# A decoder layer on Trainium2: queries moved into the stacked layout as one tile and then three

## The reference

```python
qkv = jnp.einsum('bsd,ed->bse', x, Wqkv_w) + Wqkv_b
q = qkv[..., :D_MODEL]
k = qkv[..., D_MODEL:D_MODEL + HEAD_DIM]
v = qkv[..., D_MODEL + HEAD_DIM:]
q = q.reshape(B, S, HEADS, HEAD_DIM)
scores = jnp.einsum('bqhd,bkd->bhqk', q, k) * scale
scores = jnp.where(causal[None, None], scores, min_val)
attn = jax.nn.softmax(scores, axis=-1)
ctx = jnp.einsum('bhqk,bkd->bqhd', attn, v)
...
x = x + _L0_attn_ref(_layernorm(x, axis=-1), ...)
x = x + _L0_xattn_ref(_layernorm(x, axis=-1), fside_BxS2xS2_0, ctx_1024)
x = x + _L0_ffn_ref(_layernorm(x, axis=-1), ...)
```

## Time and profile before

| | us |
|---|---|
| median of 3 runs (941.45 to 944.6) | 943.83 |
| the profiled execution | 943.11 |
| its span in the profile | 941.4 |
| PE busy in it | 902.0 |
| DVE / ACT / POOL busy | 552.4 / 338.5 / 309.5 |

### The profile page before, as it was taken

One profiled execution on the slowest core, in us unless ns is written; L12 is line 12 of the kernel. 1 busy time (PEld: TensorE's weight loads), 2 busy tenths in 40 slices (PEclk: granted clock), 3 DMA queues, 4 the chain that ended last, 5 costly groups with the idle time before them and its releaser, 6 DMA issues.

```text
span 941.4 us, 13548 instructions
## 1 busy us (share of the span) xinstructions
PE 902.0 (96%) x5191; PEld 667.7 (71%) x5191; DVE 552.4 (59%) x897; ACT 338.5 (36%) x577; POOL 309.5 (33%) x419
## 2 busy tenths in 40 slices
PE   3989998899999999999999999999999999999998
PEld 2756567655578886766688767766778778688886
DVE  2635558888557777654757768644577654422223
ACT  4333633545734153254433161434234332121110
POOL 3535733247731241235501333152323141011110
PEclk9977999899999999999999999999999999999999
DMA  9867854545856634356248334373444445265442
GB/s 310 266 207 256 301 190 129 171 142 211 307 224 175 218 129 150 130 201 240 117 174 251 134 106 161 132 290 108 163 159 162 168 180 206 91 242 194 170 179 95
DMA packets 44964, 175.07 MB, mean 186 GB/s; under 512 B 7196, under 2 KB 10268, under 8 KB 34916
## 3 DMA queue, kind: packets, MB, share of 16 engines
q1 hardware_dynamic: 35780, 114.96, 34.8%
q10 hardware_dynamic: 9120, 59.25, 17.7%
HBM read 127.46 MB, written 33.75 MB: 171 GB/s over the span
## 4 chain that ended last, share of the span: by engine, by line
PE 84%; DVE 7%; SPq 3%; ACT 2%; issue 2%; DMA 2%; POOL 0%; ACTq 0%; DVEq 0%
PE ring L1056 13%; PE ring L1058 13%; PE ring L1057 13%; PE slots L1129 4%; PE slots L1146 4%; PE av L1164 4%; PE ring L1296 4%; PE den L1164 3%; PE slots L1056 3%; PE slots L1058 3%; PE slots L1057 3%; SPq L642 2%; PE slots L1233 2%; PE ring L1053 2%; PE slots L1126 2%
## 5 line engine op out<-in xcount | busy, mean ns | idle before, releaser
L815 POOL TENSOR_TENSOR hd_l<-hd,hd_h 128x512 fp32r<-128x512 f32 x44 | 58.3, 1324 | 298.3 <-ACT hd_h L1023 298.3
L1056 PE MATMUL ring<-xT_h,gu 128*128 128x512 f32 x352 | 142.2, 404 | 0.0
L1058 PE MATMUL ring<-xT_h,gu 128*128 128x512 f32 x352 | 137.6, 391 | 0.0
L1057 PE MATMUL ring<-xT_l,gu 128*128 128x512 f32 x352 | 137.6, 391 | 0.0
L1409 DVE TENSOR_REDUCE negm<-slots 128x1 f32<-128x384 f32 (+3 forms) x176 | 106.4, 636 | 43.5 <-PE slots L1129 42.0
L931 ACT ACTIVATE probs<-slots 128x512 f32<-128x512 f32 (+1 forms) x176 | 90.0, 560 | 91.5 <-PE slots L1146 91.2
L782 POOL TENSOR_SCALAR_AFFINE_SELECT probs<-probs 128x128 f32<-128x128 f32 (+2 forms) x176 | 61.9, 361 | 132.7 <-ACT probs L931 130.7
L1129 PE MATMUL slots<-kst,qst 97*128 97x128 f32 (+3 forms) x256 | 77.7, 374 | 0.0
L1056 PEld LDWEIGHTS ring<-xT_h,gu 128*128 128x128 f32 x352 | 66.3, 188 | 15.2 <-issue 3.3
L1019 ACT ACTIVATE gated<-ring 128x512 f32<-128x512 f32 x44 | 26.3, 597 | 140.1 <-PE ring L1296 136.2
L1058 PEld LDWEIGHTS ring<-xT_h,gu 128*128 128x128 f32 x352 | 66.1, 188 | 14.5
(11 more groups left out here) (212 smaller groups left out, 1789.2 us busy)
## 6 DMA issues: line engine op xcount, KB each, us to landing
gu<-gu_parts ACTq DMA_DIRECT2D x42, 1280.0 KB, 5.5
dn<-dn_parts SPq DMA_DIRECT2D x12, 1728.0 KB, 7.2
gu_parts<-gu SPq DMA_DIRECT2D x11, 1280.0 KB, 5.7
qst<-qT_h SPq DMA_DIRECT2D x128, 64.0 KB, 2.1
raw_gu<-gu SPq DMA_DIRECT2D x11, 640.0 KB, 7.2
dn_parts<-dn SPq DMA_DIRECT2D x11, 576.0 KB, 6.6
...
```

What stands on the lines that cost most here:

```text
L815: pool.tensor_tensor(hd_l[:, i, :], hd[:, i, :], hd_h[:, i, :].bitcast(F32), ALU.subtract).then_inc(hd_lo.sem, 1)
L1056: pe.matmul(out_, w_hi_, m_hi_, start=start, stop=False, skip_group_check=True)
L1057: pe.matmul(out_, w_hi_, m_lo_, start=False, stop=False, skip_group_check=True)
L1058: return pe.matmul(out_, w_lo_, m_hi_, start=False, stop=stop, skip_group_check=True)
```

## The change

The moves of a batch become 25 transfers. The filler is one transfer for all 16 heads. Tile 0 moves as before: eight high halves in step q 0 on SP, four low ones in q 1 on ACT. Tiles 1 to 3 move together: SP issues in q 3, and ACT in v, transfers that carry one head of each of the three tiles (32 partitions x 3 x 512 numbers, 192 KB), eight high and four low. q_moved has two signals, one for tile 0 (13 transfers) and one for tiles 1 to 3 (12); the maxima of groups 1, 2 and 3 wait for the second. TURNS is another list, with 1,824 characters for 1,832 and 324 fills for 329.

```diff
--- before.py
+++ after.py
@@ -304,23 +304,23 @@
 
 
 TURNS = (
-    "AAAAAAAAA6AAAAAAWAAX2X1WX9XXXXAXXXXXXAXWXXX3XWXXXW6XX91AXAAXXAAAXXAAAA1AAWXAAWXAAAAAW4A2AWXWXX5AWXXXAAAXXAXXXA"
-    "XXAAAAAAAWXAAAAWAAAAAA79AAAAWAAAWAAA4AAAAAWAAAWAAAAAAA99AAAAAAAAAWAAAWAAAAAAAALALA2L5ALWLLLL5AWALAALLLWL15XXXX"
-    "93LL1XXLXXLLLXLLLAXAWLXL995AWXXXXLXLLL9AAAXXXX4XLLLLXXAALXLLLWXXLLL31ALLALAXWAALXXL8AALAAAA1XW9LLLWXLAALAAAXL8"
-    "XLAAXLAAALAL9AAXAAAXLLXLAAX94XLLLWLLWLLAWLLLAALXAXLXXLXAAAAAA2W8ALAAAAAAWALLLAAAAALWAALLAAWAAF6FALAAAAFAAAFAAA"
-    "ALFWWWALAFAAALLLFAFAAFALLAALAFFAFFFFLAALLAFAAFFFXFXFLXLXXFLFFFFFFFLXFXAFFXXXFFFXXXFFFLFFFFFFFLXXFFLLLXLFXFF2FF"
-    "FFAFFFFFLFFLFLXFXALLLFAFLXFXXFFALLFFLFFXAXLLLAXFFLFFXFALFFFLAFFLFFAFLFFFLLFLFLFXFLLLLAFFFLLXFFAFAALFLFFFFLAAXF"
-    "FXXFXXFFLAFAXXFFFFFFFAXFALLFFLFFXFXXFLFFXFFFAFFLFAALLFAFFAAFLAFFFFLLAFAFAFFFFAAAAAALAFLFLAFAXFXFLLFXLAALFAFFAL"
-    "AFLFAFLXAFLLLFFAFALFFAFFAALLFLAAFLAAFFFAFAFFLFFAAFLALFALFFALFFFFAAAAAFFLAAFFAAAAAFAAFAAAAFFFFLLAAFAFLAFFLAAAFF"
-    "LLFLLFFFFFFFAFFFFFFAALFFFFLAAFFALAAFXFXXFFXXFLFFLFXFFXXFFFLFXXXFXAFFXXAFFFXFFLLLFFFFAFFFAXXFFFLLLFFFXXFFXXFFXL"
-    "FFXFFXLLFLAFLXLLLFXAFFFFFAFFFLFLALFLAAAAFAALLFXFFFFLAALFLALFLAALAAFAAALFXFLLFLFFLFLFLLXFXLFFFFLLFFFLFFFFFFFLFF"
-    "FLFLXLFFFLFLLXLLXAAFLFXFFFLFFFLLFFFFAFLXFXFXFLLFFXFFFXLFXFLFLFFFFLLXLFFFLFALLLFAFAALFFAXAFFXFFFAALLLFALFXFFLFF"
-    "ALLLLFFAAAFFAFFFFAAAFAAFLLLFFFLFAAAFFFFFFFFAFFAAFFFAAFFFAAAAAAFFAAAAFAFFFAAAFAFLLLFAAFAAAAAFFAFAAFFFAAFAFAFAAF"
-    "FAFFAFFFFFFFFFAFFFFFLLFFLFFLFFFLFFFLLFLFFFF9FFFLLFLF4LLFFFFFLFLFFFLFFLFFLFFFLLLFFFFLFFFLFFFLFFFLLFFLLFFFFFLLLL"
-    "FFFFLFLLFFFLLFFLFFLFLFFFLLLFFFLFLFFFFFFFFLFLLFFFFLFLFLLLFFFFLLFLFFFFFLLFFFFFLFLFFLFFFLFFLLFLLFFFFLFLLLLFLFFFFF"
-    "FFFFFLFFLLFLFFFFLFFFLFLLLLFFFFFFFFFFFFFFFFFFFFFFFF4F94F5FFFFF7FFFFFFFFFFFFFFFFFFFFFFFFFF994FFFFFFFFFFFFFFFFFFF"
-    "F94FFFFFFFFFFFFFFFFFFFFFFFFFFFFFFFFFFFFFFFFFFFFFLFFFFFFFFFFFFFFFFF94FFFFFFFFFFFFFFFFFFFFFFFFFFFFFFFLFFFFFFFFF9"
-    "FFL4FFFFFFFFFFFFFFFFFFFFFFFFFFFFFFFFFFFFFFFFFFFFFFFLFFFLFFFFFF2FFFFFFFFF")
+    "AAAAAAAAAAA6AAAAAAXXWWXXXXAXXXXX8A994XWXXXWXXWXXXXXXAAXXAXXAAAAXXXAAAAAWAAWAXXAXAAAAAAXX91AAAAAXAXAAAAXXAWAXWA"
+    "AXWAXXAAAWAAXA29AAAAAAAAAAAAWAAAAWAAAAAAAAAAWW8AAAAAAAAAAAAWAWWAAAAWAAALALA5AWLWWLLLLLLAAALLLLA9LLXLWLLLLXLLAX"
+    "XX8XXXLAXLXXLLLL9995A91XLXLLLXX7XAXXWXAXX4AXXAALLLALWLLLLWXAALALAALXAA9AAALLXX94LLWLWXLXAAWLAAXLAWWAXLXA5X9XLL"
+    "A4AAXAAXAXLAAALAALALXLAWXALLAALALLLXA5LALLLXLLX4AXX5AAAAALLLLAAAAAALWAAAALALWAALAAAFWL5AFFAAAAAAAFAAFALAAFLAAF"
+    "AALWFLLWLAAAAFALAFFLAFFFWLAAFAALAFFFFFFFXXXFFXXFXLFFFLLFLLFFXFFAFFXLX91XXFFFFFLLFFLFFLFFAXLLXFLFXF1FFLXXAFLFLL"
+    "XFXXFFFFLFALAFFFLFFLLALLFXFXXFFFLXFXXXFLLFAFFAFLLAFFFFFLFFLFAAAFLFFXLLLAAFLLLFFFAAXAFFFLLFALXLAXXFA6FFFFAFFFLL"
+    "LAXAFFFLAXFXAFAFXAFFFFLLLXFFALFLAFAXFFLFFLXAFXFLFFFAAFFAFFXLFFFFXLAXAFFFXFLLFXFLAFAAFALFAFALALAFLFFLFLLFFAFFFA"
+    "LAALFFAAAFFLFALLAFAFFAFFFAAFFLFFAFAFFFAALALFLFFAFFFAAALLLFFFFFFFAAAFFFAAAAAAFAFAAAAFFFLFAAALFFFLFFFAFAFLLAFALF"
+    "LFAFFFFFFAALFFFFFFAAAFFFLALAFFFFFFLFXFAXXXFLLFFFFFFXFXFXXFXFLXFXFFFLFFFAXXFLLLFXLFXFFFXXFFFFFLFLFALFLALLFLFFXX"
+    "FLXAFFFFFFXFFFLXFALFLXFFLLLLFFAAFFLFLAFFLLFFFFLFLFLLXFFLLAAALFLFFFLLLFFAAFAXAAFALLFAFXFLFAFFALFLFFLFAFFFXLFFXX"
+    "LFFLXFFLLFXLFFXLFAAAFLXFLFFFFLLAXALFFFFXLFAFFFLLLFFLLFLFFFFLLFFFFXXFFLXFXXFAFAAAAAFAAAAAFLXXLXFFFAFFFFFAFFFAFF"
+    "FFAFFXFFAFFAFAFAAAFFFAAAAAAAFAAALAFAAFLLLAAFLFLFAFFAFFAAALAFAA5FAAFAAAAAFFFFLAFFAFFFFFAFFFFFAFFAFFFFAAAFLLLLLL"
+    "FFFFFLFFAFFFFLFFFFLLFLFLLLFFFFFFFFFF94FFLFLLFFLFFFLFFLFLFFFFLLLFLFLFLFLFFFFFFFFFLFFFLFFFFFLLLLFFFFFLFLLLFFFFLL"
+    "FFFLFFLLLLFFLLFFLFFLFFLFFFFFLFFFFLFFLLLFFFFFLLFLFLFFLLFFFFFLFLFFLFLFFFFFLFFLFFLFFLFLLFLFFFLFFLLLFFFLFFFLFFLFFL"
+    "FFFFFFFFFFFFFLFFFLLLLLLLFFFFFFFFFFFFFFFFFFF4F94FF5FFFF7FFFFFFFFFFFFFFFFFFFFFFFFFF994FFFFFFFFFFFFFFFFFFFF94FFFF"
+    "FFFFFFFFFFFFFFFFFFFFFFFFFLLLFFFFFFFFFFFFFFFFFFFFFFFFFFFFFFFFF94FFFFFFFFFFFFFFFFFFFFFFFFFFFFFFFFFFFFFFFFFFFFFFF"
+    "FFF94FFFFFFFFFFFFFFFFFFFFFFFFFFFFFFFFFFFFFFFFLFFFFFFLFFFFFFFFFFF")
 
 
 def streams_of():
@@ -498,7 +498,7 @@
         kv_ps, kv_act, kv_lo = sig("kv_ps"), sig("kv_act", 3), sig("kv_lo")
         q_ps, q_hi, q_lo = sig("q_ps", KT), sig("q_hi", KT), sig("q_lo", KT)
         v_ps, v_ready = sig("v_ps"), sig("v_ready")
-        q_moved, m_moved = [sig(f"q_moved{i}", 16 * 13) for i in range(KT)], [sig(f"m_moved{i}", 32) for i in range(4)]
+        q_moved, m_moved = [sig(f"q_moved{i}", 16 * (13 - i)) for i in range(2)], [sig(f"m_moved{i}", 32) for i in range(4)]
         s_ps, s_max = sig("s_ps", 4 * MG), sig("s_max", 4 * MG)
         m_ps, m_hi, m_lo = sig("m_ps", 4), sig("m_hi", 4), sig("m_lo", 4)
         t_ps, p_exp, p_ready = (sig(name, SCORES_TO[-1]) for name in ("t_ps", "p_exp", "p_ready"))
@@ -532,6 +532,15 @@
         ad_ps, ad_added = sig("ad_ps", len(SEGMENTS)), sig("ad_added", len(SEGMENTS))
         out_ps, out_added = sig("out_ps", TT * len(SEGMENTS)), sig("out_added", TT * len(SEGMENTS))
         ff_link = sig("ff_link", FF_LINKS)
+
+        def tiles_moved(e):
+
+            return slice(0, 1) if e == 0 else slice(1, KT)
+
+        def moved_heads(row, e, j):
+
+            heads = qst[row:row + HD, :, :].bitcast(F32).rearrange("p (e j) t -> p e j t", j=4)
+            return heads[:, tiles_moved(e), j, :]
 
         def product_of(b, n):
 
@@ -631,16 +640,19 @@
                     sp.dma_start(wqkv_l[:, :, :].bitcast(F32), parts[:, 1]).then_inc(wqkv_loaded.sem, 16)
 
             def q(b, e):
-                if b == 0 and e < 2:
-                    sp.wait_ge(w_lo.sem, KT)
-                elif b and e == 0:
-                    sp.wait_ge(o_ps.sem, o_ps.at(b - 1, 2))
-                sp.dma_start(qst[KROWS:MROW, 4 * e:4 * e + 4, :].bitcast(F32), mask_r[0:4 * TT, 0, :].bitcast(F32)).then_inc(q_moved[e].sem, 16)
+                if e == 0:
+                    if b == 0:
+                        sp.wait_ge(w_lo.sem, KT)
+                    else:
+                        sp.wait_ge(o_ps.sem, o_ps.at(b - 1, 2))
+                    sp.dma_start(qst[KROWS:MROW, :, :].bitcast(F32), mask_r[0:HEADS * TT, 0, :].bitcast(F32)).then_inc(q_moved[0].sem, 16)
+                if e not in (0, KT - 1):
+                    return
                 sp.wait_ge(q_hi.sem, q_hi.at(b, e + 1))
                 for row in (0, 2 * HD):
                     for j in range(4):
-                        sp.dma_start(qst[row:row + HD, 4 * e + j, :].bitcast(F32), qT_h[HD * j:HD * j + HD, e, :].bitcast(F32))\
-                          .then_inc(q_moved[e].sem, 16)
+                        sp.dma_start(moved_heads(row, e, j), qT_h[HD * j:HD * j + HD, tiles_moved(e), :].bitcast(F32))\
+                          .then_inc(q_moved[min(e, 1)].sem, 16)
 
             def rows_(b, g):
                 sp.wait_ge(m_hi.sem, m_hi.at(b, g + 1))
@@ -896,22 +908,22 @@
                 if b and e == 0:
                     act.wait_ge(pv_done.sem, pv_done.at(b - 1, 16))
                 act.activation(qT_h[:, e, :], ps[:, 0, :], ACT.Identity, bias=bq_sb[:, e:e + 1]).then_inc(q_hi.sem, 1)
-                if e:
-                    low_rows(b, e - 1)
+                if e == 1:
+                    low_rows(b, 0)
 
             def v_(b):
                 low_rows(b, KT - 1)
 
             def low_rows(b, e):
 
-                if b == 0 and e < 2:
+                if b == 0:
                     act.wait_ge(w_lo.sem, KT)
-                elif b and e == 0:
+                elif e == 0:
                     act.wait_ge(o_ps.sem, o_ps.at(b - 1, 2))
                 act.wait_ge(q_lo.sem, q_lo.at(b, e + 1))
                 for j in range(4):
-                    act.dma_start(qst[HD:2 * HD, 4 * e + j, :].bitcast(F32), qT_l[HD * j:HD * j + HD, e, :].bitcast(F32))\
-                       .then_inc(q_moved[e].sem, 16)
+                    act.dma_start(moved_heads(HD, e, j), qT_l[HD * j:HD * j + HD, tiles_moved(e), :].bitcast(F32))\
+                       .then_inc(q_moved[min(e, 1)].sem, 16)
 
             def rows_(b, g):
                 act.wait_ge(m_ps.sem, m_ps.at(b, g + 1))
@@ -926,8 +938,8 @@
                 if step >= 2:
                     act.wait_ge(pv_done.sem, pv_done.at(b, step - 1))
                 elif step == 0 and unit == 0:
-                    for e in range(KT):
-                        act.wait_ge(q_moved[e].sem, q_moved[e].at(b, q_moved[e].per))
+                    for moved in q_moved:
+                        act.wait_ge(moved.sem, moved.at(b, moved.per))
                 act.activation(probs[:, at:at + heads, 0:n], slot("scores", b, step, unit)[:, 0, 0:heads * n].rearrange("p (h n) -> p h n", n=n),
                                ACT.Exp, scale=SCALE).then_inc(p_exp.sem, 1)
 
@@ -1118,7 +1130,8 @@
                     if b == 0:
                         pe.wait_ge(consts_ready.sem, 6)
                 if i == 0:
-                    pe.wait_ge(q_moved[g].sem, q_moved[g].at(b, q_moved[g].per))
+                    for moved in q_moved[min(g, 1):min(g, 1) + 1]:
```

(1 more changed line is left out.)

## The result

The changed kernel takes 945.23 us (median; 940.43 to 947.39), the kernel before 941.22 us (938.32 to 944.60) beside it: a ratio of 1.0031 [1.0017, 1.0045]. The forecast of 936.8 us was wrong in sign: the change costs 0.3%, about as much as can be told from nothing. The 20 times of the changed kernel fall into two groups, 940.4 to 942.0 and 944.6 to 947.4 us, so that one execution can lie 4 us from the median. The profiled execution took 945.34 us with a span of 943.6, against 943.11 and 941.4 before.

The account below looks back on a forecast made before the run. TensorE was held in batch 0 by the order of SP's queue. From 943.1 us, -4.6 (first scores product) - 2.3 (rest of batch 0) + 0 (batch 1) + 2.0 - 1.4 (batches 2, 3) = -6.3 gave 936.8 us; range 929 to 947.5.

Parts of the forecast that it names:

- What bounds it: Batch 0: SP's queue order delays the row maxima, so the first scores product starts only at 56.94 us.
- The landing: Batch 0, tiles 1 to 3: 2.36 MB from 34.3 us, landing at 44.2 us, called the unknown.
- the three prices: Landing of batch 0's tiles: 47.3 us at 205 GB/s, 44.2 at 280, 41.4 at 424; 44.2 taken.
- Issue: Batch 0: 0.62 us per SP transfer, queries done at 39.3 us, row maxima landing near 47 us at worst.
- First scores product: Batch 0: starts at 52.3 us in place of 56.94, 4.6 us earlier, if the tiles landed at 44.2.
- too late: Rival, group 1's first maxima, batches 0 and 1: tiles late, 6.2 us lost in each, 949.2 us; chance 0.22.
- The rest of batch 0: First scores product to output projection: 29 fills for 50, 2.3 us less; up to 9.9 more by the clock.
- more than forecast: Rival, batch 0: the clock stays up, 6 to 9 us further gain, 928 to 931 us; chance 0.11.
- Batch 1: 134 fills for 135, VectorE's work unchanged: priced at zero, from 4 us gained to 6 us lost.
- Batches 2 and 3: From 264 us on: 18 more fills cost 2.0 us, against 1.4 us less waiting ahead of batch 3.
- The 1.43 us of the earlier trace: PE's wait at 519.16 us, ahead of batch 3's first scores product: 1.4 us less, between nothing and that.
- behind 264 us the feed-forward covers the moves: Batches 2 and 3: feed-forward work hides the transfers, so what they can save lies in batches 0 and 1.

Follow-up runs that it names:

- e4_own_signal: The changed kernel, but tile 1 moves alone with its own signal, tiles 2 and 3 together behind it (37 transfers); 942.42 us, 1.0007 of the kernel before.
- e5_own_two: The changed kernel, but tile 1 has its own transfers and signal in batches 0 and 1 only; 934.98 us, 0.9930 of the kernel before.
- e7_fewer_bytes: The changed kernel, but in batches 1 to 3 four of twelve three-tile copies carry one tile; 939.75 us, 0.9983 of the kernel before.
- e1_old_order: The changed kernel's 25 transfers in the order of the kernel before (329 fills); 982.16 us, 1.0428 of the kernel before.
- e8_own_one: The changed kernel, but tile 1 has its own transfers and signal in batch 0 only; 938.35 us, 0.9978 of the kernel before.
- e6_w_earlier: The old 52 transfers in the changed kernel's order, with batch 2's w_raw load ahead of the third tile's transfers; 939.78 us, 0.9981 of the kernel before.

## Why the prediction was wrong, point by point

*What bounds it: right.* The order of SP's queue held the first scores product; with the row maxima off that path PE no longer waits for them, and where the tiles are in time too (e4_own_signal, e5_own_two) it starts at 54.9 to 55.1 us and not 56.94. With the new order and the old 52 transfers (e2_new_order) PE still waits 4.65 us for the row maxima.

*The landing: the step that failed.* The three tiles were to land at 44.2 us, at 280 GB/s, and PE went on at 47.70. From the 35.8 us at which their bytes were to start, 2.36 MB in 11.9 us are 198 GB/s over all, so the lowest of the three prices (205 GB/s, 47.3 us) came near and the one that I took did not. The 280 was 205 GB/s divided by the engines' share of 73%, over 26 to 34 us. That stretch mixes two kinds of copy, as two pieces of it in the kernel before show:

```profile
26.00:28.00 2.00, 2.00 (x11) 1.63 (x10) 0.75 (x1) 0.04 (x1) 0.00 (x0) 1.00 0.79 288
30.00:32.00 2.00, 2.00 (x10) 1.65 (x9) 0.43 (x1) 0.69 (x1) 2.00 (x3) 1.00 0.85 207
```

Up to 28 us the end of the loads of x is in it, which are faster. From 30 to 32 us, with queries alone on both queues, it is 207 GB/s at a share of 0.85, and the same division gives 243 GB/s and a landing at 45.5 us: 1.3 of the 3.5 us that were missing. The rest is that the copies were slower still at a full share (222 to 234 GB/s over 10 us), and that a few packets came behind the others: from 36 us on, 2.36 MB at 234 GB/s end at 46.1 us, and from 46 to 47.7 us only 19 packets under 8 KB begin. Why these are late, no run shows.

*Issue: mis-sized.* SP was to be done with the queries at 39.3 us and was at 42.08, ACT was to need 0.71 us for a transfer and needed 1.17: three times the bytes do not issue at the price of one when the engines are behind. The row maxima left when forecast (43.85 us) but took 8.3 to 8.7 us to land and were there from 52.5 us on, not near 47: hardly in time for a scores product at 52.3 us.

*First scores product: forecast 52.3, measured 59.82 us.* The 7.5 us are 0.3 (fills end at 44.51, where 44.2 was the start), 3.2 (the wait) and 4.0: group 1's maxima were to take 8.1 us from there and took 12.1, at a granted clock of 0.50 from 50 to 60 us. The rival "too late" had priced 3.1 + 3.1 us. Without the wait, in e5_own_two, the product still comes 2.8 us later than forecast, at a clock of 0.82 in the 10 us before it: part of the slow clock was not the wait's, and the forecast had taken none.

*The rest of batch 0: forecast -2.3, measured -8.2 us.* The fills are the 29 counted. The other 6 us are the clock, 0.92 for 0.85: the rival "more than forecast", priced at 6 to 9 us, came for this stage while "too late" came for the one before it. I had taken the two for alternatives. The same code also took 62.63 us at 0.84 in the execution of e7_fewer_bytes, and the old list 62.70 us at 0.92 in that of e1_old_order, so of these 6 us not much is sure, and their coming here is in part luck.

*Batch 1: forecast 0, measured +2.9 us.* The rival's price there was 6.2 us; e5_own_two against e8_own_one shows 6.0. In the changed kernel half of it is hidden by what the new order gains in this batch otherwise: without the wait the stage falls to 137.46 us, 3.5 under the kernel before.

*Batches 2 and 3: forecast +0.6, measured +4.5 us.* The fills cost what was said: 2 became 17 in the fourth stage, 2.38 us for 0.39. The 1.43 us of the earlier trace rows did not come back as a gain, since a wait of 1.01 us for the tiles stands at the same place. And the cover failed: PE, never idle in that stage before, now idles 2.15 us, 1.55 of them for row maxima of batch 2. That wait is 1.83 us with 52 transfers too (e6_w_earlier): it is the order's. That "behind 264 us the feed-forward covers the moves" did not hold either, for a queue that also brings the load of w_raw (e2_new_order: 11.86 us).

*Sum.* By the same four steps the rival "too late" would have had +1.6, -2.3, +6.2 and +0.6, together +6.1 us; measured were +2.9, -8.2, +2.9 and +4.5. It was the right mechanism in both places it named. Against its sum the rest of batch 0 came out 5.9 us lower, by its clock, and batch 1 3.3 us lower, the other two steps 1.3 and 3.9 us higher. And the forecast started from the 943.1 us of one execution, where the kernel before took 941.2 us beside the changed one: the time was missed by 8.4 us, the change itself by 10.3 (+4.0 for -6.3).
